# Neighbour counts compared four at a time and summed by GpSimd, residual of six groups moved to GpSimd

## The reference

```python
x = x + L0(x)     # gated causal averages, then a layer norm over channels
x = x + L1(x)     # attention, sparse or dense by row of the batch
```

```python
s_scores = einsum('bhsd,bhskd->bhsk', Q, K[:, :, idx]) * scale
s_scores = where(prior_index_mask, s_scores, -inf)
sparse_out = einsum('bhsk,bhskd->bhsd', softmax(s_scores), V[:, :, idx])
```

## Time and profile before

| | us |
|---|---|
| median of 3 runs | 341.86 (341.52 to 347.49) |
| profiled execution, its own time | 341.25 |
| its span, first to last instruction | 339.3 |
| TensorE busy | 317.3 (93%) |
| VectorE busy | 291.6 (86%) |
| GpSimd busy | 224.3 (66%) |
| ScalarE busy | 215.0 (63%) |

### The profile page before, as it was taken

The page is one execution under the profiler, slowest core; times in us unless marked ns, Lnnn a source line. Parts: engine busy times, 40 slices in busy tenths (PEclk is TensorE's granted clock), DMA queues, the critical chain, the costliest instruction groups (busy, mean ns, idle before and its releaser), DMA issues. The chain is left out here.

```text
span 339.3 us, 10025 instructions
## 1 busy us (share of the span) xinstructions
PE 317.3 (93%) x3333; PEld 211.4 (62%) x3333; DVE 291.6 (86%) x1500; ACT 215.0 (63%) x458; POOL 224.3 (66%) x279
## 2 busy tenths in 40 slices
PE   7998888999999999999988799999999999999995
PEld 2545254573756557474535576777787877787873
DVE  3895699999898999988788866999999999999982
ACT  6760225566455656555716787788888878888863
POOL 3254164535355453625537768799999999999990
PEclk9996799999999999999999999999999999999999
DMA  6600002015060421301551244565555354301011
GB/s 190 198 3 0 31 0 65 32 49 93 2 139 2 90 52 53 88 0 53 69 74 28 39 93 79 84 120 139 127 100 122 92 123 101 84 5 34 2 34 33
DMA packets 29155, 23.08 MB, mean 68 GB/s; under 512 B 2736, under 2 KB 27824, under 8 KB 29104
## 3 DMA queue, kind: packets, MB, share of 16 engines
q1 hardware_dynamic: 29104, 22.44, 30.3%
HBM read 7.75 MB, written 2.10 MB: 29 GB/s over the span
## 5 line engine op out<-in xcount | busy, mean ns | idle before, releaser
L1566 POOL TENSOR_TENSOR arena<-arena,neg_max 128x512 f32<-128x512 f32 x128 | 129.6, 1042 | 14.3 <-DVE neg_max L1437 13.8
L1437 DVE CUSTOM_DVE_ANT_0 arena<-ps,arena 128x128 f32<-128x128 f32 x512 | 113.6, 286 | 11.6 <-issue 5.8
L1076 ACT ACTIVATE arena<-ps 128x512 f32<-128x512 f32 x128 | 69.6, 597 | 9.0 <-PE ps L775 8.9
L1514 POOL TENSOR_TENSOR arena<-arena 128x448 f32<-128x448 f32 (+6 forms) x56 | 41.1, 735 | 48.5 <-DVE arena L1268 45.1
L775 PE MATMUL ps<-ident_sb,arena 128*128 128x128 f32 x512 | 68.2, 276 | 0.0
L775 PEld LDWEIGHTS ps<-ident_sb,arena 128*128 128x128 f32 x512 | 56.5, 141 | 7.0 <-issue 4.3
L1501 POOL TENSOR_TENSOR arena<-decay_a,arena 128x192 f32<-128x192 f32 x32 | 20.0, 655 | 36.2 <-ACT arena L920 36.2
L1437 DVE DVE_READ_ACCUMULATOR2_ANT neg_max<- 128x1 f32 x512 | 42.4, 83 | 0.0
L791 PE MATMUL ps<-arena 128*32 128x128 f32 x1024 | 41.2, 279 | 0.0
L791 PEld LDWEIGHTS ps<-arena 128*32 128x32 f32 x1024 | 24.0, 109 | 6.9 <-issue 0.3
L761 PE MATMUL ps<-arena 48*128 48x128 bf16 x512 | 25.4, 219 | 3.0 <-DVE neg_max L1437 3.0
(11 more groups left out here) (164 smaller groups left out, 584.2 us busy)
## 6 DMA issues: line engine op xcount, KB each, us to landing
arena<-q_parts SPq DMA_DIRECT2D x96, 64.0 KB
arena<-k_parts SPq DMA_DIRECT2D x96, 64.0 KB
arena<-in_x SPq DMA_DIRECT2D x16, 256.0 KB, 3.7
arena<-in_xt SPq DMA_DIRECT2D x8, 256.0 KB, 3.6
out<-arena SPq DMA_DIRECT2D x7, 256.0 KB, 3.5
arena<-in_consts SPq DMA_DIRECT2D x1, 420.0 KB, 3.7
w_sb<-in_w SPq DMA_DIRECT2D x1, 384.0 KB, 5.2
w_sb<-in_w SPq DMA_DIRECT2D x1, 192.0 KB, 4.3
```

The costliest lines, as they stand in the source:

```text
L1076: act.activation(probT[q % PT_RING], ps[1][:, q % 2, :], ACT.Exp, scale=-1.0)\
L1437: dve.tensor_tensor_reduce(out=neg_t[q % NT_RING][:, cs], in0=ps[0][:, score_bank(c) + slot, cs], in1=nbias[n % 2], scale=1.0, scalar=3.0e ...
L1514: pool.tensor_tensor(a, a, pr_, ALU.add).then_inc(s["lag_added"], 1)
L1566: pool.tensor_tensor(t4, t4, neg_max[:, n % 2, 4 * z:4 * z + 4].unsqueeze(2).broadcast_to([P, 4, P]), ALU.subtract).then_inc(s["shifted"], 1)
```

## The change

Three things, all in the first stage.

1. **Counts.** The index table is written as bf16 (`idx_b`). One VectorE instruction now compares 4 indices with the 128 keys, 128 x 512 elements of bf16, with both operands broadcast (the keys over the 4 indices, the index over the 128 keys). There are 8 of these instead of 32 that compared 128 elements and added. The first writes `so_far`, the others one of two buffers `hot`; seven GpSimd instructions (`counted`) add them to `so_far`. Steps 1 to 4 have two quads each; steps 0, 5 and 6 have none.
2. **Residual** of groups 0 to 5: GpSimd multiplies `ln` by `rstd` and adds `xb`, two instructions of 128 x 512, at the start of its step; VectorE's four are gone there. Groups 6 and 7 stay on VectorE.
3. **GpSimd's order**: the counts' sums stand between its lags, and `c_rstd` stands ahead of lag 7 instead of behind it. `late_tables` has one VectorE addition more.

```diff
-FIRST_COUNT = (0, 6, 12, 17, 22, 27, K_SPARSE, K_SPARSE)
+FIRST_QUAD = (0, 0, 2, 4, 6, 8, 8, 8)
...
-            def counts(first, last):
-
-                for j in range(first, last):
-                    n = so_far[j % 2][:]
...
-                        dve.wait_ge(s["vec_step"], vec(f"hot{j - 2}"))
-                        pro(f"hot{j}", dve.scalar_tensor_tensor(n, key_no[:], idx_m[:, j:j + 1], n,
-                                                                ALU.is_equal, ALU.add), waited=False)
+            def counts(r):
+
+                if r > 2:
+                    dve.wait_ge(s["counted"], r - 2)
+                pro(f"hot{r}", dve.tensor_tensor(so_far[:] if r == 0 else hot[r % 2],
+                                                 key_no[:].unsqueeze(1).broadcast_to([P, 4, P]),
+                                                 idx_b[:, 4 * r:4 * r + 4].unsqueeze(2).broadcast_to([P, 4, P]),
+                                                 ALU.is_equal), waited=False)
 
             def late_tables():
-                dve.wait_ge(s["vec_step"], vec(f"hot{K_SPARSE - 1}"))
-                pro("count", dve.tensor_tensor(lncnt[:], so_far[0][:], so_far[1][:], ALU.add))
+                dve.wait_ge(s["counted"], K_SPARSE // 4 - 1)
+                pro("two_counts", dve.tensor_tensor(so_far[:, 0:2, :], so_far[:, 0:2, :], so_far[:, 2:4, :], ALU.add))
+                pro("count", dve.tensor_tensor(lncnt[:], so_far[:, 0, :], so_far[:, 1, :], ALU.add))
...
                 if closes:
                     b_carries(i, m)
-                    c_residual(i, m - 1)
                     f_mod_parts(i, m + 1)
...
                 f_lags(i, m + 1, range(0, 2))
                 if first < last:
-                    counts(first, first + 2)
+                    counts(first)
                 b_temporal(i, m)
                 f_lags(i, m + 1, range(2, 4))
                 if first < last:
-                    counts(first + 2, first + 4)
+                    counts(first + 1)
                 b_mixed(i, m)
-                f_lags(i, m + 1, range(4, 6))
-                if first < last:
-                    counts(first + 4, last)
-                f_lags(i, m + 1, range(6, 7))
+                f_lags(i, m + 1, range(4, 7))
...
+            def c_residual(i, m):
+
+                u = m % 2
+                pool.wait_ge(s["centred"], grp(i, m, GB, GB))
+                pool.wait_ge(s["rstd_ready"], grp(i, m, 1, 1))
+                pool.tensor_tensor(by_row(x1g[u]), by_row(ln[u]), rstd[:, u, :].unsqueeze(2).broadcast_to([P, GB, P]),
+                                   ALU.mult).then_inc(s["scaled"], 1)
+                pool.wait_ge(s["scaled"], grp(i, m, 1, 1))
+                pool.wait_ge(s[f"xb_loaded{u}"], i * 16 + 16 * (m // 2 + 1))
+                pool.tensor_tensor(x1g[u], x1g[u], xb[u], ALU.add).then_inc(s["x1_ready"], 1)
...
             def step(i, m):
+                first, last = FIRST_QUAD[2 * i + m], FIRST_QUAD[2 * i + m + 1]
+                if not at_start(i, m, 1):
+                    c_residual(i, m - 1)
                 f_decayed(i, m + 1, range(GB))
                 if not at_start(i, m, 1):
                     c_keep(i, m - 1)
-                f_lags(i, m + 1, range(1, Q))
+                f_lags(i, m + 1, range(1, 2))
+                if first < last:
+                    counted(first)
+                f_lags(i, m + 1, range(2, 4))
+                if first < last:
+                    counted(first + 1)
+                f_lags(i, m + 1, range(4, 7))
                 c_rstd(i, m)
+                f_lags(i, m + 1, range(7, Q))
...
+            def counted(r):
+
+                if r > 0:
+                    pool.wait_ge(s["vec_step"], vec(f"hot{r}"))
+                    if r > 1:
+                        pool.wait_ge(s["counted"], r - 1)
+                    pool.tensor_tensor(so_far[:], so_far[:], hot[r % 2], ALU.add).then_inc(s["counted"], 1)
```

More of the change, by code:

```diff
@@ L73 @@
              "key_no", "idx_f", "mask_f", "idx_plus", "idx_masked", "kept_bias"] + \
-            [f"hot{j}" for j in range(K_SPARSE)] + ["count", "cnt_one", "cnt_none"]
+            [f"hot{r}" for r in range(K_SPARSE // 4)] + ["two_counts", "count", "cnt_one", "cnt_none"]
 ACT_STEPS = ["exp_tau", "softplus", "exp_table", "exp_blend", "lt", "apow", "decay_p", "decay_a", "exp_u", "w_b3", "w_a1", "w_a3"]
@@ L132, in build @@
         key_no = sb("key_no", [P, P], BF16)
-        so_far = [sb(f"so_far{k}", [P, P], BF16) for k in range(2)]
+        so_far = sb("so_far", [P, 4, P], BF16)
+        idx_b = sb("idx_b", [P, K_SPARSE], BF16)
         table_probe = sb("table_probe", [P, 1])
@@ L196, in build @@
         attnT = [take(P) for _ in range(2)]
+        hot = [a.rearrange("p (j k) -> p j k", j=4) for a in (
+            arena[:, at[0] - 4 * P:at[0] - 2 * P].bitcast(BF16), arena[:, at[0] - 2 * P:at[0]].bitcast(BF16))]
         end_at, at[0] = at[0], 0
@@ L233, in build @@
             "cross_ps cross_ready crossT_ps temporal_ready temp_ps temp_tanh mixed_ready out_ps aggr_begun "
-            "stats_ready moments_ready vareps_ready rstd_ready centred x1_ready x1b_ready half_ready const_ps kept_ready xb_loaded0 xb_loaded1 "
+            "stats_ready moments_ready vareps_ready rstd_ready centred scaled x1_ready counted x1b_ready half_ready const_ps kept_ready xb_loaded0 xb_loaded1 "
             "x1T_ps x1T_ready q_ps k_ps v_ps "
@@ L1191, in neighbours @@
                 pro("idx_plus", dve.scalar_tensor_tensor(idx_m[:], idx_f, 1.0, im_f, ALU.add, ALU.mult))
-                pro("idx_masked", dve.tensor_scalar(idx_m[:], idx_m[:], -1.0, None, ALU.add), waited=False)
+                pro("idx_masked", dve.tensor_scalar(idx_b[:], idx_m[:], -1.0, None, ALU.add))
             def early_tables():
@@ L1364, in step @@
                 closes = not at_start(i, m, 1)
-                first, last = FIRST_COUNT[2 * i + m], FIRST_COUNT[2 * i + m + 1]
+                first, last = FIRST_QUAD[2 * i + m], FIRST_QUAD[2 * i + m + 1]
                 if closes:
                     b_carries(i, m)
-                    c_residual(i, m - 1)
                     f_mod_parts(i, m + 1)
```

## The result

The changed kernel takes 340.17 us (median of 20 runs, 339.26 to 342.68), the kernel before 341.48 beside it: a ratio of 0.9966, 95% interval 0.995 to 0.9983. By that ratio it is 1.2 us less, inside the 2% and inside the range. The total was met, but three terms of its sum were wrong: one was too dear and two were too good, and they nearly cancel.

The account below looks back on a forecast made before the run. It took TensorE's matmuls plus a latency chain to bound the plain steps. On the profiled 341.25 us, -0.5 - 1.1 - 0.2 + 1.4 + 0 = -0.4 gave 340.85, put at 341.0 measured; 8-in-10 range 338.8 to 343.2.

Parts of the forecast that it names:

- Steps 3 to 5: taking work from VectorE buys nothing.: Plain steps: TensorE's matmuls and a chain of latencies set their length, so less VectorE work gains 0.
- The rival in which VectorE is the bound: The gap before lag 6 goes too, about 0.7 us in each of six steps: 334.6 us, chance 0.03.
- Step 0, -0.5: Temporal in step 0 no longer starts behind a pair of counts: 0.5 us less.
- Step 1, -1.1: The residual no longer stands before VectorE's locals, for which b_cross waits, and temporal gains another 0.2: 1.1 us less.
- Step 2, -0.2: The rest of step 1's backlog goes from step 2: 0.2 us less.
- Steps 1 to 4, +0.35 each, +1.4: GpSimd's lag 2 holds the second comparison, so mixed comes late: 0.35 us in each of four steps, 1.4 more.
- released at 102.96, it ends 0.6 later: The second comparison, held until GpSimd's lag 2 ends, then ends about 103.65, making mixed 0.35 us late.
- Step 6, 0 between -0.64 and +0.75: Missing residual gains up to 0.64 us; late tables held by GpSimd's residual cost up to 0.75; taken as 0.
- after what TensorE's lead and the missing residual absorb: Step 6: carries at worst 2.1 us late, locals with them, but only 0.75 us more than now after this absorption.
- steps 3 and 4 at 19.9: Step length in us named beforehand as a sign that the forecast holds.
- the cheap comparison: 512 bf16 elements take 0.35 us, or GpSimd's lag 2 comes second, so mixed is never late: 338.8 us, chance 0.18.
- The slower one: Exclusion bites at both comparisons, 0.6 us in each of four steps, step 6 gives 0.75: 343.1 us median, chance 0.19.

Follow-up runs that it names:

- experiment 5: The kernel before without 30 of its 32 counts, so its table of counts is not the right one: 340.67 us, ratio 0.9993.
- experiment 9: The kernel before with only TensorE's order changed, the last subtraction for q and b_out ahead of lag 6: 338.85 us, ratio 0.994.
- experiment 1: The changed kernel again, unaltered, for a second profile: 340.53 us, ratio 0.9972 to the kernel before.
- experiment 7: The changed kernel with all four late tables ahead of temporal of step 5 and `kept` near the head of step 0: 338.94 us, ratio 0.9939.
- experiment 2: The changed kernel with the late tables split and moved into step 5, two before temporal and two before mixed: 339.18 us, ratio 0.9939.
- experiment 8: The kernel of experiment 7 with the last subtraction for q and b_out ahead of lag 6 on TensorE, run twice: 334.65 and 334.62 us.
- experiments 4: The kernel before with only the residual of six groups on GpSimd and rstd ahead of lag 7: 341.47 us, ratio 0.9975.
- experiment 6: The changed kernel with the second comparison of each of steps 1 to 4 made twice: 345.29 us, ratio 1.0128.

## Why the prediction was right in total and where its steps failed

- **"Steps 3 to 5: taking work from VectorE buys nothing."** Right. They are 19.57 with full counts, with quads and, in experiment 5, with none. The rival in which VectorE is the bound is out on the old order. On the better order of experiment 9 VectorE's load costs 0.3 us a step (19.20 against 18.91). GpSimd's second sum, charged 0, cost nothing either: the moments start 18.22 us into step 3 (105.52 - 87.30), before it was 18.21 (106.25 - 88.04).
- **Step 0, -0.5.** Right: -0.49 at temporal in experiment 1, -0.48 at the start of step 1.
- **Step 1, -1.1.** Half of it: -0.54. I took the residual's 1.14 us off VectorE and didn't ask where GpSimd would do it in step 1. `kept` (0.46) stands ahead of it there, and the residual then lies against VectorE's bf16 parts. VectorE and GpSimd of the first profile after, step 1:

```profile
52.27 1.40 DVE L1247 TENSOR_TENSOR arena<-arena,mod_pa 64x512 f32<-64x512 f32 x1
53.70 0.42 DVE L1250 CAST mod_pa<-arena 64x512 bf16<-64x512 f32 x1
54.16 1.13 DVE L1252 TENSOR_TENSOR mod_pb<-arena,mod_pa 32x512 bf16<-32x512 f32 x1
```

```profile
50.19 0.46 POOL L1574 TENSOR_TENSOR kept<-kept_bias,rows_sb 128x128 f32<-128x128 f32 x1
50.72 1.04 POOL L1525 TENSOR_TENSOR arena<-arena,rstd 128x512 f32<-128x512 f32 x1
51.84 1.27 POOL L1529 TENSOR_TENSOR arena<-arena 128x512 f32<-128x512 f32 x1
54.15 2.69 POOL L1499 TENSOR_TENSOR arena<-decay_a,arena 128x192 f32<-128x192 f32 x4 [1.03 <-ACT arena L924]
```

  The first meets the residual's addition, the third the decay factors; each takes 0.69 when GpSimd is quiet. With `kept` moved (experiment 7) they take 0.85 and 0.69, and step 1 is 19.58, so the full -1.1 was there to be had.

  The larger part of it is a race, though, decided by 0.01 us. In experiment 2 `kept` stands where it did, the first instruction takes 1.39, but the third is issued just ahead of the decay factors (L1254 and L1503 there) and runs free. Step 1 is 19.76:

```profile
52.57 0.69 DVE L1254 TENSOR_TENSOR mod_pb<-arena,mod_pa 32x512 bf16<-32x512 f32 x1
```

```profile
52.58 2.79 POOL L1503 TENSOR_TENSOR arena<-decay_a,arena 128x192 f32<-128x192 f32 x4 [1.04 <-ACT arena L924]
```

  So 0.46 of the 0.56 us that are missing here can come or not from one execution to the next; with `kept` moved VectorE is 0.54 us ahead (52.96 against 53.50).
- **Step 2, -0.2.** Right: 19.81 to 19.57.
- **Steps 1 to 4, +0.35 each, +1.4.** It measured 0. The hold was there as foreseen, the second comparison 1.21 us long. The failed step is "released at 102.96, it ends 0.6 later": after its release it needed some 0.4 (102.2 to 102.64), as if part of its 0.68 had been spent while it was held. (The sentence also says 0.6 and reckons 103.65 - 102.96 = 0.69; with 0.6 the term would have been 0.25 a step, still not 0.) The tanh ends at the same time to within a tenth. This term, 0.35 us, was a difference of two instruction ends, and I had no row for a held instruction of 512 columns.
- **Step 6, 0 between -0.64 and +0.75.** It measured +1.01 (21.23 against 20.22), beyond my worst bound, and 2.37 in the profile in which the clock fell as well. I had the parts: tables before carries, held by both of GpSimd's residual instructions, carries about 2 us later (at 4.31 us, beyond the 3 that I had named as the sign that the 0 is wrong). What failed is "after what TensorE's lead and the missing residual absorb". The residual stood behind the carries, so its absence absorbs nothing for b_locals, which wait for the carries alone. The rows give the sum. Carries and b_locals of step 3 after:

```profile
88.85 2.12 DVE L1283 TENSOR_TENSOR arena<-ps,half_bw 32x512 f32<-32x512 f32 x3
```

```profile
92.20 1.13 PE L564 MATMUL ps<-arena 32*96 32x128 f32 x32
```

  In step 3 b_locals start 1.23 us behind the end of the carries (90.97); in step 6 it is 0.15 (152.44 to 152.59). So 1.08 of the 2.76 us by which the carries are later is absorbed, 1.68 is not, and 19.57 + 1.68 = 21.25 against 21.23.

The sum as measured in the steps of experiment 1 is -0.48 - 0.54 - 0.24 + 0 + 1.01 = -0.25 us, against a forecast of -0.4. The 1.4 that I charged to the plain steps stood instead in steps 1 and 6 (0.56 and 1.01). That the total came out right is luck: terms wrong by 1.4, 0.56 and 1.01 cancel to 0.15. Of the recorded signs, steps 3 and 4 at 19.9 and step 1 at 19.7 to 20.0 didn't come. By the ratio the kernels differ by 1.2 us (interval 0.6 to 1.7), the profiled executions of before and of experiment 1 by 0.5. Runs of one kernel scatter by over 1 us and each kernel has one or two profiles; where the other 0.7 us lie stays open.

The exclusion that the Trainium skill states (SBUF — State Buffer, "SBUF: two separate sides") agrees with these rows, L1218 at 1.21 against 0.68 and L1247 at 1.40 against 0.69. It also names VectorE's two-port performance modes, which I passed over; the one-tensor L1227, 1.24 against 0.23 in experiment 7, fits that.

Of the rivals, the cheap comparison is out: 0.68 us free, not 0.35. The slower one didn't come either: the first comparison runs free and mixed is late in no step. Only its price for step 6 came, 1.01 where it had 0.75.

## What to carry to other kernels

When work moves from one engine to a neighbour that excludes it, write down for each place what the neighbour will be doing then. The rare places (first step, last step, a table built once) cost more here than the four plain steps that the change was about. A wait's slack belongs to one consumer: ask for each consumer which of the removed work really stood ahead of it.

Before an engine is relieved, find out whether the gap of the bound engine is load or latency. A run without the work (experiment 5) shows which. A latency gap is closed by other work of the bound engine, moved into it (experiment 8, 0.66 us a step), and only then does the relieved engine's load count.

## What the hardware showed beyond that

- The same pause of TensorE, 1.61 us at the same place, was followed once by a granted clock of 0.91 and 0.75 over the next two stretches of 5 us, and once by 1.00 throughout. In the first case a group of four 128 x 128 transposes (L425, at 155.41) took 1.06 us where it takes 0.60 in the second. Step 6 was 1.36 us longer for it. It isn't a matter of this place. A pause of 1.70 or 1.71 us stands early in the attention of all twelve profiles, and only in those of experiments 4 and 7 does the clock fall behind it, to 0.50 for some 3 us; their attention takes 173.2 and 173.3 us where it takes 172.2. Experiment 7:

```profile
191.00:193.00 2.00, 2.00 (x12) 1.93 (x11) 0.82 (x6) 1.47 (x3) 2.00 (x4) 0.50 0.60 82
```

  Experiment 2, whose profile has no pause in step 6 and no fall there or in the attention, still has five of its twelve runs at a mean granted clock of 0.979 and 339.8 to 340.4 us, and seven at 0.987 to 0.989 and 338.0 to 339.6. Why the clock falls in one execution and not in another, the profiles don't show.
- A comparison held by GpSimd ends 0.4 to 0.6 us behind the release although it takes 0.68 by itself: 0.40 in step 3, 0.40 and 0.56 for the two of experiment 6 (lags 2 and 3 there started at 102.38 and took 2.21 together). The ends of GpSimd's instructions are the softest numbers in this.
- The next instruction can start late although the one in front of it shows only 0.21 us (count_none in experiment 2, read above as held by GpSimd). The releaser then named, the tanh, had ended 0.47 us before.
- GpSimd's instructions of 128 x 512 aren't alike: 1.04 us where one number of the second operand serves 128 columns, as in `ln` times `rstd` (L1525) and in the attention's subtraction; 1.27 for the addition of two full f32 tensors (L1529) and for the kept copy, whose second operand is the same 128 columns for each of the 4 rows (L1535); and 1.15 for the bf16 sums (L1582). The residual is thus 2.4 us on GpSimd (50.72 to 53.11) and not the 2.1 of the prediction.
